# Decay attention in steps of half the tokens, with the values of two pairs of heads projected together

## What is computed

```python
qkv = jax.nn.silu(x @ qkv_w.T)            # 32 heads, each q, k, v of 64
for each block of 32 tokens, in order:
    aw = (q_i @ k_j.T) * decay            # inside the block
    out = aw @ v_j + (q_i * qd) @ state   # and from the blocks before
    state = state * bd + (k_j * kd).T @ v_j
attn = rmsnorm(out over all 2048 columns) * norm_w
gate = jax.nn.sigmoid(x @ gate_w.T)
y = (gate * attn) @ out_w.T
```

## Time and profile before

| | |
|---|---|
| median of 3 runs | 1226.85 us |
| the profiled execution | 1225.85 us |
| its span | 1224.0 us |
| the 16 pairs, from PE's first product to its last | 388.13 us |
| PE, DVE, ACT, POOL busy in them | 386.45, 156.13, 175.02, 137.28 us |
| granted clock of PE in them | 1.00 |

### The profile page before, as it was taken

How to read it: one execution, slowest core, us unless ns; L and a number is a source line. 1 busy time by engine, 2 the same in 40 slices (tenths; PEclk the granted TensorE clock), 3 DMA queues, 4 the chain that set the end, 5 groups by cost and what they waited for, 6 DMA issues and landing times. The chain is left out here.

```text
span 1224.0 us, 22142 instructions
## 1 busy us (share of the span) xinstructions
PE 1096.9 (90%) x7357; PEld 884.7 (72%) x7370; DVE 711.7 (58%) x1590; ACT 513.6 (42%) x1133; POOL 319.1 (26%) x390
## 2 busy tenths in 40 slices
PE   9999899898999999999999978989898976699980
PEld 6667566565788888888888756868686852699980
DVE  2455576677533443344334367878787854488855
ACT  3433134353454345444544424434343432466640
POOL 3000040000232433343333314444443424000005
PEclk9999999998999999999999989999999998799995
DMA  4000000001111011111111010000010034765513
GB/s 154 1 1 0 0 22 2 1 0 58 63 56 35 34 47 56 34 34 47 56 34 34 35 40 18 23 5 34 0 39 0 17 129 159 254 221 202 203 56 112
DMA packets 25324, 70.81 MB, mean 58 GB/s; under 512 B 2752, under 2 KB 15296, under 8 KB 23104
## 3 DMA queue, kind: packets, MB, share of 16 engines
q1 hardware_dynamic: 23744, 66.05, 15.4%
q0 software_dynamic: 1536, 4.20, 1.1%
HBM read 59.23 MB, written 11.01 MB: 57 GB/s over the span
## 5 line engine op out<-in xcount | busy, mean ns | idle before, releaser
L993 DVE TENSOR_TENSOR d_s_m<-ps,d_decay 128x384 f32<-128x384 f32 x128 | 71.2, 556 | 118.1 <-PE ps L1083 116.3
L124 PE MATMUL ps<-warm 128*128 128x512 bf16 x346 | 87.7, 409 | 14.6 <-PEq L902 4.8
L1347 ACT ACTIVATE e_probs<-ps,e_neg_max 128x128 f32<-128x128 f32 (+1 forms) x128 | 52.8, 417 | 112.7 <-DVE e_neg_max L1294 112.7
L124 PEld LDWEIGHTS ps<-warm 128*128 128x128 bf16 x358 | 36.5, 104 | 59.2 <-issue 25.4
L1037 ACT ACTIVATE d_gated_hi<-d_gated 128x256 fp32r<-128x256 f32 x64 | 26.7, 417 | 125.3 <-DVE d_gated L974 125.3
L115 PE MATMUL ps<-xTl,d_wh 128*128 128x512 f32 x192 | 77.6, 404 | 0.6
L115 PE MATMUL ps<-xTh,d_wl 128*128 128x512 f32 x192 | 75.9, 395 | 0.0
L115 PE MATMUL ps<-xTh,d_wh 128*128 128x512 f32 x192 | 75.9, 395 | 0.0
L115 PE MATMUL ps<-wl_gated,f_wh 128*128 128x256 f32 x240 | 69.3, 289 | 3.2 <-DVE wl_gated L1651 2.0
L750 ACT ACTIVATE g_probs<-ps,g_neg_max 128x128 f32<-128x128 f32 (+1 forms) x128 | 46.9, 418 | 55.7 <-DVE g_neg_max L706 55.4
L960 POOL TENSOR_TENSOR d_sq_sum<-d_sq_sum,d_sq 128x256 f32<-128x256 f32 x64 | 47.4, 740 | 82.6 <-ACT d_sq L1039 82.6
(11 more groups left out here) (350 smaller groups left out, 3267.8 us busy)
## 6 DMA issues: line engine op xcount, KB each, us to landing
f_stage<-in_w_experts SPq DMA_DIRECT2D x15, 1536.0 KB, 6.6
d_stage<-in_w_decay SPq DMA_DIRECT2D x17, 640.5 KB, 3.8
d_decay<-in_decay SPq DMA_DIRECT2D x16, 384.0 KB, 3.0
slot_rows<-warm SPq DMA_DIRECT2D x1, 3840.0 KB, 12.8
slot_outs<-f_rows SPq DMA_DIRECT2D x15, 256.0 KB, 2.2
e_stage<-in_w_grouped SPq DMA_DIRECT2D x5, 640.0 KB, 3.9
e_wo<-in_wo_grouped SPq DMA_DIRECT2D x5, 512.0 KB, 3.6
f_rows<-slot_rows SPq DMA_DIRECT2D x1, 2560.0 KB, 14.5
```

The lines of the kernel that those rows point to most:

```text
L124: pe.matmul(out, c.warm16[:, 0:P], c.warm16[:, 0:out.shape[1]], start=True, stop=True)
L993: dve.tensor_tensor(s_m[:, s % 4, :], ps[:, 4 + s % 2, 0:CAUSAL], decay[:, s % 2, :], ALU.mult).then_inc(sm_ready, 1)
L1347: act.activation(probs[:, t % 4, cols], bank[:, cols], ACT.Exp, bias=neg_max[:, t % 4, b:b + 1], accum_out=sums[:, t % 4, b:b + 1]).then_i ...
```

## The change

The stage runs in 32 steps instead of 16 pairs: step s works on pair s % 16 and half s // 16 of the tokens, that is two of the four batches. All buffers over tokens have half their size. The code is written out step by step in place of a loop.

- PE in a step: scores of both batches, with the two heads issued pass by pass; the gate product; values times weights of both batches; queries and keys of the next step; in every second step the values of two pairs, as a split product with activations stationary and the weights of both pairs, 256 columns, moving; the output projection of the step.
- Scores have four banks (2 to 5), gate and result one each (7, 6), the output sums two (0, 1). The sums of the first half are copied out at step 16 and their norm and residual are done in step 18; the second half's at the end.
- DVE masks both heads of a batch in one instruction (768 columns, two banks). Its other operations and ACT's run once a step over 512 tokens.
- The weights are loaded in four pieces (queries and keys, gate, output, and values of two pairs), each once its place is split, and each half of the tokens loads and splits all of them again; so do the decay tables.

```diff
-        self.wv = sb("wv", [P, KD, P])
+        self.stage_v = sb("stage_v", [P, KD, 2, P])
+        self.wvh = sb("wvh", [P, KD, 2, P], F32R)
+        self.wvl = sb("wvl", [P, KD, 2, P], F32R)
...
+    def load_qk(self, sp, n):
+        cols = slice(0, 2 * P)
+        source = self.projections(self.c.dram["w_decay"][n % PAIRS][:, 0:self.PROJ], cols)
+        sp.dma_start(self.projections(self.stage[:, 0:self.PROJ], cols), source).then_inc(self.qk_in, 16)
...
+    def load_v(self, sp, n):
+        for j in range(2):
+            source = self.projections(self.c.dram["w_decay"][(2 * n + j) % PAIRS][:, 0:self.PROJ], slice(3 * P, 4 * P))
+            sp.dma_start(self.stage_v[:, :, j, :], source).then_inc(self.v_in, 16)
...
+    def split_qk(self, pool, n):
+        qk = self.projections(self.stage[:, 0:self.PROJ], slice(0, 2 * P))
+        wh, wl = self.wh[:, :, 0:2 * P], self.wl[:, :, 0:2 * P]
+        pool.wait_ge(self.qk_in, 16 * (n + 1))
+        pool.tensor_tensor(wh, qk, self.nought[:].unsqueeze(1).broadcast_to((P, KD, 2 * P)), ALU.add).then_inc(self.qk_high, 1)
+        pool.wait_ge(self.qk_high, n + 1)
+        pool.tensor_tensor(wl, qk, wh.bitcast(F32), ALU.subtract).then_inc(self.qk_split, 1)
...
+    def split_v(self, pool, n):
+        stage, wh, wl = (t[:].rearrange("p k j n -> p (k j n)") for t in (self.stage_v, self.wvh, self.wvl))
+        pool.wait_ge(self.v_in, 32 * (n + 1))
+        pool.tensor_tensor(wh, stage, self.nought[:].broadcast_to((P, KD * 2 * P)), ALU.add).then_inc(self.v_high, 1)
+        pool.wait_ge(self.v_high, n + 1)
+        pool.tensor_tensor(wl, stage, wh.bitcast(F32), ALU.subtract).then_inc(self.v_split, 1)
...
-    def split(self, pool, n):
-
-        nought = self.nought[:].unsqueeze(1)
-        stage = self.stage[:, 0:self.PROJ].rearrange("p (k n) -> p k n", k=KD)
-        pool.tensor_tensor(self.wh[:], stage[:, :, 0:3 * P], nought.broadcast_to((P, KD, 3 * P)), ALU.add).then_inc(self.w_hi, 1)
-        pool.tensor_tensor(self.wv[:], stage[:, :, 3 * P:], nought.broadcast_to((P, KD, P)), ALU.add)
-        pool.wait_ge(self.w_hi, n)
...
+    def prepare(self, pool):
+        pool.memset(self.nought[:], 0.0).then_inc(self.zeroed, 1)
+        pool.wait_ge(self.zeroed, 1)
+        self.split_qk(pool, 0)
+        self.split_v(pool, 0)
+        self.split_g(pool, 0)
+        self.split_o(pool, 0)
...
+    HALF = TOK // 2
+    STEPS = 2 * PAIRS
...
-            with pool.Fori(0, PAIRS) as i:
-                pool.wait_ge(proj_ps, LEAD + 8 * i + 8)
-                pool.wait_ge(stage_in, 16 * i + 16)
-                pre.split(pool, i + 2)
-                for b in range(BATCH):
-                    pool.wait_ge(sq_ready, LEAD + BATCH * i + b + 1)
-                    pool.wait_ge(sq_added, LEAD + BATCH * i + b - 3)
-                    cols = slice(b * SEQ, (b + 1) * SEQ)
-                    pool.tensor_tensor(sq_sum[:, cols], sq_sum[:, cols], sq[:, b % 2, :], ALU.add).then_inc(sq_added, 1)
-                pool.wait_ge(op_ps, LEAD + BATCH * (i + 1))
+            pool.wait_ge(qk_ps, 2)
+            pre.split_qk(pool, 1)
+            for s in range(STEPS):
+                if s + 1 < STEPS:
+                    pool.wait_ge(g_ps, s + 1)
+                    pre.split_g(pool, s + 1)
+                if s + 2 < STEPS:
+                    pool.wait_ge(qk_ps, 2 * s + 4)
+                    pre.split_qk(pool, s + 2)
+                if s + 1 < STEPS:
+                    pool.wait_ge(op_ps, s + 1)
+                    pre.split_o(pool, s + 1)
+                if s % 2 == 0 and s + 2 < STEPS:
+                    pool.wait_ge(v_ps, s + 2)
+                    pre.split_v(pool, s // 2 + 1)
+                cols = slice(s // PAIRS * HALF, (s // PAIRS + 1) * HALF)
+                pool.wait_ge(sq_ready, s + 1)
+                pool.tensor_tensor(sq_sum[:, cols], sq_sum[:, cols], sq[:], ALU.add).then_inc(sq_added, 1)
...
-            with sp.Fori(0, PAIRS - 1) as i:
-                sp.wait_ge(sm_ready, LEAD + 8 * i + 8)
-                sp.dma_start(decay[:], c.dram["decay"][bass.ds(i + 1, 1)].rearrange("a p h s -> p (a h) s")).then_inc(decay_in, 16)
-                sp.wait_ge(pre.wo_split, i + 2)
-                sp.dma_start(stage[:], c.dram["w_decay"][bass.ds(i + 2, 1)].rearrange("a p n -> p (a n)")).then_inc(stage_in, 16)
+            for s in range(STEPS):
+                if s + 1 < STEPS:
+                    sp.wait_ge(sm_ready, 2 * s + 2)
+                    sp.dma_start(decay[:], c.dram["decay"][(s + 1) % PAIRS]).then_inc(decay_in, 16)
+                if s + 2 < STEPS:
+                    sp.wait_ge(pre.qk_split, s + 2)
+                    pre.load_qk(sp, s + 2)
+                    sp.wait_ge(pre.g_split, s + 2)
+                    pre.load_g(sp, s + 2)
+                    sp.wait_ge(pre.o_split, s + 2)
+                    pre.load_o(sp, s + 2)
+                if s % 2 == 1 and s + 3 < STEPS:
+                    sp.wait_ge(pre.v_split, s // 2 + 2)
+                    pre.load_v(sp, s // 2 + 2)
...
+            def mask(s, b):
+                dve.wait_ge(s_ps, 2 * s + b + 1)
+                if b == 0:
+                    dve.wait_ge(decay_in, 16 * (s + 1))
+                    need(dve, pv_ps, s)
+                dve.tensor_tensor(s_m[:, 2 * b:2 * b + 2, :], ps[:, 2 + 2 * b:4 + 2 * b, 0:CAUSAL], decay[:], ALU.mult).then_inc(sm_ready, 1)
...
+            for s in range(STEPS):
+                mask(s, 0)
+                mask(s, 1)
+                gate_out(s)
+                if s == PAIRS + 2:
+                    variance(0)
+                low_out(s)
+                if s + 1 < STEPS:
+                    low_queries(s + 1)
+                    low_keys(s + 1)
+                if s == PAIRS + 2:
+                    scale(0)
+                    dve.wait_ge(acc_out, 2)
+                    for t in range(4):
+                        dve.scalar_tensor_tensor(c.y[:, t, :], c.y[:, t, :], stat[:, 0, t:t + 1], c.x[:, t, :], ALU.mult, ALU.add)
...
+            for s in range(STEPS):
+                if s == PAIRS:
+                    act.wait_ge(op_ps, PAIRS)
+                    for bank in range(2):
+                        act.activation(c.y[:, 2 * bank:2 * bank + 2, :].rearrange("p t d -> p (t d)"), ps[:, bank, :], ACT.Copy).then_inc(acc_out, 1)
+                act.wait_ge(g_ps, s + 1)
+                act.activation(gate[:], ps[:, GATE_OF, :], ACT.Tanh, scale=0.5).then_inc(g_out, 1)
+                act.wait_ge(og_ready, s + 1)
+                need(act, op_ps, s)
+                act.activation(gated_hi[:], gated[:], ACT.Copy).then_inc(out_hi, 1)
+                if s + 1 < STEPS:
+                    queries(s + 1)
+                    keys(s + 1)
+                    if s % 2 == 1:
+                        values_of(s // 2 + 1)
+                need(act, sq_added, s)
+                act.activation(sq[:], ps[:, VALUES_OF, :], ACT.Square).then_inc(sq_ready, 1)
+                if s == PAIRS + 2:
+                    root(0)
...
-                        for t in range(4):
-                            tok = slice((n % 2 * 4 + t) * P, (n % 2 * 4 + t + 1) * P)
-                            for k in range(KD):
-                                mm = pe.matmul(bank[:, t * P:(t + 1) * P], c.xT[:, k, tok], wv[:, k, :], start=(k == 0), stop=(k == KD - 1))
...
-                for step in range(BATCH + 2):
-                    if step < BATCH:
-                        scores(2 * step)
-                        scores(2 * step + 1)
-                    if 1 <= step <= BATCH:
-                        values(step - 1)
-                    if step >= 2:
-                        project(step - 2)
...
+            def values_in(n):
+                pe.wait_ge(pre.v_split, n + 1)
+                first = tokens(2 * n).start
+                for b in range(2):
+                    for t in (2 * b, 2 * b + 1):
+                        cols = slice(first + t * P, first + (t + 1) * P)
+                        mm = split_product(pe, ps[:, 3 + 2 * b, t % 2 * D:(t % 2 + 1) * D], lambda k: c.xTh[:, k, cols], lambda k: c.xTl[:, k, cols],
+                                           lambda k: wvh[:, k].rearrange("p j n -> p (j n)"), lambda k: wvl[:, k].rearrange("p j n -> p (j n)"), range(KD))
+                    mm.then_inc(v_ps, 1)
...
+            def scores(s):
+                if s == PAIRS + 3:
+                    pe.wait_ge(var_ready, 1)
+                pe.wait_ge(qk_lo, 2 * s + 2)
+                pe.wait_ge(v_out, 2 * (s // 2) + 2)
+                for b in range(2):
+                    heads = [(ps[:, 2 + 2 * b + h, :], slice(h * HD1, (h + 1) * HD1)) for h in range(2)]
+                    queries, late = slice(b * SEQ, (b + 1) * SEQ), slice(b * SEQ + P, (b + 1) * SEQ)
+                    for n, (k, q) in enumerate(((k_hi, q_lo), (k_lo, q_hi), (k_hi, q_hi))):
+                        for bank, rows in heads:
```

(22 more changed lines are left out.)

318 lines of the change are left out of this document (152 added, 166 removed).

## The result

The changed kernel took 1181.21 us, the median of 4 runs (1179.74 to 1181.8), beside 1226.51 us for the kernel before in the same session (1226.09 to 1227.27): a ratio of 0.9633, with a 95% interval of 0.962 to 0.9645, or 45.3 us less. The forecast was 1178.0 in a range of 1158 to 1200. The profiled execution took 1181.48 (span 1179.6), which is 44.4 under that of before (1225.85); the forecast's sum had 48.8.

A forecast was written before the change was run, and what follows sets the result against it. PE's own queue was taken to bound the decay attention stage. 52.3 us gained over 16 pairs less 3.5 once-only gives 48.8 off 1225.85: 1177.1, or 1178.1 by the median; forecast 1178 us, range 1158 to 1200.

The forecast's parts named there:

- what the wait on the keys' low half adds: Before the next scores in steps without values, only the output projection covers 1.76 us, so scores start 0.12 us late.
- first wait, copies, squares: One-time PE costs: 0.85 us for Silu of the values, 0.2 for copies delaying ACT, 1.0 for the squares' product.
- VectorE's stop in the middle: At the change of halves, DVE's root with table loads and four result tiles costs PE 2.0 us.
- the prediction's own signs of being wrong: In the decay attention stage: scores of 1 us a batch, PE waits on splits, or a granted clock under 1.00.
- The change of tile: On PE, switching kinds of array tile costs 0.24 us; four a step instead of about 13 a pair.
- the rival of fewer gaps: A change of array tile on PE costs only 0.10 us, giving 20.0 a pair and 1162 us; chance 0.15.
- The heads: Both heads' scores, issued pass by pass, fully share PE's array: 0.585 us a batch, 1.17 a step.
- The price of the rival: Heads overlap no better than before: scores 2.04 us a step, 20 us more, 1198 us; chance 0.10.
- DMA: nothing: Weight loads on SP's one queue, read twice in four pieces, land in time and cost PE nothing.
- POOL becomes the bound: POOL's in-order splits hold PE if durations grow; at 1.6 times, 28 us more, 1255 us; chance 0.05.
- DVE is held by POOL: DVE's low-half subtractions each wait for a POOL instruction, up to 1.3 us: 21 us more, 1199 us; chance 0.08.
- The masks: DVE's score masks cost nothing, covered by the gate product; without it about 1 us a step would stand bare.

The follow-up runs named there:

- the run with the hold: Kernel with reordered loads and spread result tiles (1173.51 us), plus POOL holding its next query/key weight split until the keys' low half is made: 1169.97 us, ratio 0.9537.

## Why the prediction was right, and by which steps it was off

**What holds.** The time of 1181.2 lies in the range, and the main mechanism, PE's own queue with cheaper scores and fewer changes of tile, is what the trace shows. That it came within 3.2 us of the forecast is partly luck: 4.6 us more were gained in the steps than forecast and 1.9 outside the stage, against 4.3 more lost in the middle and 6.6 on POOL. From the steps, in the profiled execution:

| Term | Predicted | Measured |
|---|---|---|
| two steps, undisturbed | 20.99 | 20.70 |
| gain over 16 pairs | 52.3 | 56.9 |
| step without values | 9.15 | 9.07 |
| scores of a step, with their change of tile | 1.41 | 1.37 |
| all changes of tile in a step | 0.96 | 8.82 - 8.07 = 0.75 |
| values' product | 2.81 | 2.80 |
| what the wait on the keys' low half adds | 0.12 | 9.07 - 8.82 = 0.25 |
| first wait, copies, squares | 0.85, 0.2, 1.0 | 0.78, 0.2, 0.93 |
| VectorE's stop in the middle | 2.0 | 6.25 |
| end | -0.6 | -0.4 (remainder) |
| PE waiting for POOL's split | 0 | 6.6 |

Copies, squares, the stop and POOL's waits are read as the excess of single steps over 9.07 or 11.62 (9.27, 10.00, 17.87, and nine steps of 12.21 to 12.87). In the stage that makes 56.9 - 7.8 - 6.6 = 42.5 where 48.8 was forecast; with the 1.9 outside it, 44.4. Two of the prediction's own signs of being wrong came: PE waited for splits, and the granted clock fell under 1.00 in the stage, in the middle.

**The change of tile** was put at 0.24; PE's own step of 8.82 less the matmuls' 8.07 leaves 0.75, 0.19 each. It lies between the forecast and the rival of fewer gaps (0.10), and is 6.7 us less in 32 steps than forecast; the wait on the keys' low half took 2.1 of them back.

**The heads.** The forecast's 1.17 a step was right, its reason only in part: the order alone is 0.45 of the 2.29 us that the scores gave a pair. The price of the rival (20 us if the change does not do what it says) was too high: with the heads in turn the scores cost 1.59 a step, not 2.04. And 1.02 was not what a batch cost before. It was read from one batch; the 64 took 80.2 us, 1.25 each. This did not harm the sum, which counts the new step and takes it from the 24.26 of the whole old pair, but it hid what the four banks were worth.

**"DMA: nothing"** was the step that failed, 6.6 us. I worked out the loads' times along one path, each issued once its own place was free, and did not ask what stands ahead of it in SP's queue. Nine steps with values were 0.6 to 1.3 longer, of which the waits are 4.2 and the slow start behind each of them about 0.25. With the queue reordered and POOL's work unchanged, none of the steps with values but the one in the middle is longer than 11.63. POOL's work was put at 16 us of 21 and is 259 in 342, the same share. The rival "POOL becomes the bound" took the wrong cause, its durations; the place, a split behind the output projection of its step, was right.

**"DVE is held by POOL"** happens, against what I read from the earlier trace rows. In the kernel before each of the 64 subtractions of 414 to 427 ns ran beside one of POOL's additions, but for 0.02 to 0.19 us only, at the end of the one that had started first; queries' and keys' low halves met nothing on POOL. In the changed kernel, count and ns least, median, most of the keys' low half:

```profile
L1035 DVE TENSOR_TENSOR wl_gated<-d_k_T,wh_gated x32: 419/526/1505, 317.5 to 652.3; 128x256 fp32r<-128x256 f32 x32
```

It cost little here (2.8 us of waits in all, and 14 times the 0.18 that is due anyway makes 2.5 of them) only because the slow ones fell mostly into steps with values, where the product covers them. Once the loads were early it was 3.5 us, as the run with the hold shows. The Trainium skill (SBUF — State Buffer, "SBUF: two separate sides") says that VectorE with two SBUF inputs and GpSimd take a shared pair of ports as a lock for a whole instruction, whoever starts first. By this rule, the trace agrees: of the two instructions above each late starter was lengthened, by 0.40 and 0.26, and neither early one for that. The sizes follow too, but for a constant. Where a low half on VectorE began inside an instruction of POOL in the changed kernel (39 times in the stage), it was longer by the time that POOL still had to run less 0.13 to 0.15 us: 0.40 left gave 0.26, 0.55 gave 0.41, 0.86 gave 0.72, 1.22 gave 1.08. In the kernel before 16 began so, with 0.11 to 0.13 left, and none was longer. That is why its rows showed next to nothing, though the rule held.

**The stop in the middle** was 2.0 in the sum. Two things were missing. The result tiles were taken near the 0.40 of the earlier trace rows, where one operand lies in PSUM; with both in SBUF and POOL beside them they took 3.86 for four (0.48 is the least for one, in the run with the hold). And PE, after 3.75 us at rest, got half its clock, which the forecast had not counted: 2.5 us more.

**The masks** are covered by the gate product, as said; the price of "about 1 us a step" without it was only half of what its place is worth (38 us in 32 steps), since the gate's Tanh also heads the chain to the next scores. This price stood in no sum.
